# Channel attention: the negated, turned maxima are kept by ScalarE, between its exponentials, and counted on a semaphore of their own

## The reference, cut to what matters

```python
def _L1_xattn_ref(qkv, y):          # qkv: the layer-normed x, y: ctx_2048, both (32, 64, 256)
    N_HEADS = 16
    bs, width, length = qkv.shape   # 32, 64, 256
    ch = width // N_HEADS           # 4
    q = qkv.reshape(bs * N_HEADS, ch, length)
    k = v = y.reshape(bs * N_HEADS, ch, -1)
    scale = 1.0 / math.sqrt(math.sqrt(ch))
    weight = jnp.einsum('bct,bcs->bts', q * scale, k * scale)
    weight = jax.nn.softmax(weight.astype(jnp.float32), axis=-1).astype(weight.dtype)
    a = jnp.einsum('bts,bcs->bct', weight, v)
    return a.reshape(bs, -1, length)
...
    x = x + _L1_xattn_ref(_layernorm(x, axis=-1), ctx_2048)
```

## Time and profile before

| | us |
|---|---|
| median of 3 runs | 2005.89 (2004.52 to 2006.66) |
| the profiled execution, its own time | 2003.32 |
| its span, first to last instruction | 2001.5 |
| VectorE busy in the span | 1536.0 (77%) |
| TensorE busy (matmuls) | 1693.3 (85%) |
| ScalarE busy | 1030.8 (52%) |
| the reductions L1481, 256 of 1218 ns | 304.7 |
| the exponentials L1464, 512 of 598 ns | 278.6 |

### The profile page before, as it was taken

One profiled execution on the slowest core, in us unless ns is written; L12 is line 12 of the kernel. 1 busy time (PEld: TensorE's weight loads), 2 busy tenths in 40 slices (PEclk: granted clock), 3 DMA queues, 4 the chain that ended last, 5 costly groups with the idle time before them and its releaser, 6 DMA issues. The chain is left out here.

```text
span 2001.5 us, 43208 instructions
## 1 busy us (share of the span) xinstructions
PE 1693.3 (85%) x15683; PEld 999.4 (50%) x15744; DVE 1536.0 (77%) x2859; ACT 1030.8 (52%) x2056; POOL 741.9 (37%) x939
## 2 busy tenths in 40 slices
PE   5999999599999999787846763777777599999998
PEld 2665665267777677744424440222222146656565
DVE  5766666689989899669977987999999268675754
ACT  3666665255555555333316752888888333323222
POOL 4644321586777667387652333122221000000000
PEclk9999999799999999989979995999999799999999
DMA  9601000200000000011201111121211013222222
GB/s 240 165 28 49 28 7 2 62 14 9 15 12 9 6 9 1 22 53 54 63 16 33 40 29 30 47 62 53 58 55 40 24 39 92 90 70 69 67 78 53
DMA packets 86797, 94.91 MB, mean 47 GB/s; under 512 B 17472, under 2 KB 63168, under 8 KB 86592
## 3 DMA queue, kind: packets, MB, share of 16 engines
q1 hardware_dynamic: 82848, 87.76, 15.8%
q10 hardware_dynamic: 2976, 2.32, 0.5%
q0 software_dynamic: 768, 2.10, 0.4%
HBM read 78.51 MB, written 10.22 MB: 44 GB/s over the span
## 5 line engine op out<-in xcount | busy, mean ns | idle before, releaser
L205 PE MATMUL ps<-arena 128*128 128x512 f16 (+6 forms) x6403 | 1093.1, 324 | 81.1 <-POOL arena L1076 20.2
L205 PEld LDWEIGHTS ps<-arena 128*128 128x128 f16 (+1 forms) x6464 | 603.3, 99 | 471.1 <-issue 45.1
L1464 ACT ACTIVATE arena<-ps 128x512 f32<-128x512 f32 x512 | 278.6, 598 | 84.2 <-PE ps L1402 61.1
L1481 DVE TENSOR_REDUCE arena<-ps 128x4 f32<-128x1024 f32 x256 | 304.7, 1218 | 22.2 <-PE ps L1394 22.2
L1394 PE MATMUL ps<-arena 31*128 31x256 f16 x1024 | 103.5, 279 | 90.2 <-ACT arena L1464 53.6
L1449 PE MATMUL ps<-arena 128*32 128x256 f32 x2048 | 164.1, 392 | 2.6 <-ACT arena L1471 0.6
L2217 DVE TENSOR_TENSOR arena<-ps,arena 128x512 f32<-128x512 f32 x96 | 66.2, 690 | 117.5 <-ACT arena L2090 95.1
L2090 ACT ACTIVATE arena<-ps 128x512 f32<-128x512 f32 x96 | 57.2, 596 | 183.4 <-PE ps L205 183.1
L1394 PEld LDWEIGHTS ps<-arena 31*128 31x128 f16 x1024 | 34.9, 92 | 206.8 <-DVE arena L1481 153.0
L968 POOL TENSOR_TENSOR arena<-arena 128x512 f32<-128x512 f32 x96 | 98.6, 1041 | 44.8 <-DVE arena L156 43.7
L571 POOL TENSOR_TENSOR arena<-arena 128x256 f32<-128x256 f32 x64 | 39.2, 612 | 187.3 <-DVE arena L541 187.3
(11 more groups left out here) (200 smaller groups left out, 3009.0 us busy)
## 6 DMA issues: line engine op xcount, KB each, us to landing
arena<-moe_cw SPq DMA_DIRECT2D x64, 192.0 KB, 2.9
arena<-moe_cw SPq DMA_DIRECT2D x64, 128.0 KB, 3.0
arena<-in_L_ffn_gate_up_proj SPq DMA_DIRECT2D x12, 512.0 KB, 3.9
ch_out<-arena SPq DMA_DIRECT2D x32, 128.0 KB
arena<-moe_cw SPq DMA_DIRECT2D x64, 64.0 KB, 2.8
arena<-in_L_ffn_down_proj SPq DMA_DIRECT2D x6, 512.0 KB, 3.6
ch_keys<-arena SPq DMA_DIRECT2D x48, 64.0 KB, 2.0
arena<-ch_keys SPq DMA_DIRECT2D x64, 48.0 KB
```

Source lines behind the costliest of these rows:

```text
L205: last = nc.tensor.matmul(out, a, b, start=start and n == 0, stop=stop and n == len(pairs) - 1, skip_group_check=not group)
L1464: nc.scalar.activation(pT[:, b % 3, g], ps[:, T[n % len(T)], :].rearrange("p (u t) -> p u t", u=KD), ACT.Exp, scale=CH_SCALE).then_inc(s_e ...
L1481: nc.vector.tensor_reduce(m[:, half % 2, 2 * half_pair:2 * half_pair + 2, j, :], ps[:, bank(user):bank(user) + 2, :].rearrange("p g (u s) ...
```

## The change

The negation of the turned maxima leaves VectorE's list and enters ScalarE's, as a copy with scale -1. It counts on a new semaphore, `s_turned`; `s_maxed` counts reductions alone. A function `free` turns "user u is done with" into the right wait: for a turned user on `s_turned`, for the others on `s_maxed`, less the turned ones before it. SyncE's `load_max` waits for `s_turned`. ScalarE's loop begins two slots earlier, so that the copy of half h stands at slot b = 4h - 2, behind exponential g = 1.

```diff
+    turn_users = [a_turn(half) for half in range(CH_HALVES)]
+
+    def free(pe, user):
+
+        earlier = sum(u <= user for u in turn_users)
+        if user in turn_users:
+            pe.wait_ge(s_turned, earlier)
+        else:
+            pe.wait_ge(s_maxed, user + 1 - earlier)
@@ SyncE
             def load_max(half):
-                sp.wait_ge(s_maxed, a_turn(half) + 1)
+                sp.wait_ge(s_turned, half + 1)
@@ TensorE
                     user = (a_first, a_second)[pair](t)
                     if user >= 2:
-                        pe.wait_ge(s_maxed, user - 1)
+                        free(pe, user - 2)
...
                     user = a_turn(half)
-                    pe.wait_ge(s_maxed, max(user - 1, a_second(t - 1) + 1))
+                    free(pe, user - 2)
+                    free(pe, a_second(t - 1))
@@ ScalarE
-            for b in range(CH_SLOTS + CH_HALF):
+            for b in range(-2, CH_SLOTS + CH_HALF):
                 for g in range(CH_RGS):
-                    if b < CH_SLOTS:
+                    if 0 <= b < CH_SLOTS:
...
+                    half = (b + 2) // CH_HALF
+                    if g == 1 and (b + 2) % CH_HALF == 0 and half < CH_HALVES:
+                        user = a_turn(half)
+                        act.wait_ge(s_scored, user + 1)
+                        if half >= 2:
+                            act.wait_ge(m_in[half % 2], 16 * (half // 2))
+                        nc.scalar.activation(mT[:, half % 2], ps[0:32, bank(user), 0:P], ACT.Copy, scale=-1.0).then_inc(s_turned, 1)
@@ VectorE
                     top(a_first(t), t, 0)
-                if t % CH_HALF == 0 and t > 0:
-                    half = t // CH_HALF - 1
-                    user = a_turn(half)
-                    dve.wait_ge(s_scored, user + 1)
-                    if half >= 2:
-                        dve.wait_ge(m_in[half % 2], 16 * (half // 2))
-                    nc.vector.tensor_scalar(mT[:, half % 2], ps[0:32, bank(user), 0:P], -1.0, None, ALU.mult).then_inc(s_maxed, 1)
                 if t < CH_SLOTS:
                     top(a_second(t), t, 1)
```

More of the change, by code:

```diff
@@ L1291, in channel_stage @@
     s_norm, s_hi, s_lo, s_vset, s_ones, s_zero = (sem(c) for c in ("norm", "hi", "lo", "vset", "ones", "zero"))
-    s_scored, s_maxed, s_scoredT, s_exped, s_mixed, s_okept = (sem(c) for c in ("scored", "maxed", "scoredT", "exped", "mixed", "okept"))
+    s_turned, s_scored, s_maxed, s_scoredT, s_exped, s_mixed, s_okept = (sem(c) for c in ("turned", "scored", "maxed", "scoredT", "exped", "mixed", "okept"))
     s_inverse, s_divided, s_finished = sem("inverse"), sem("divided"), sem("finished")
```

## The result

The change makes the kernel slower, as forecast: 2023.26 us (2022.74 to 2026.09, 4 runs) against 2005.20 (2003.77 to 2006.66), ratio 1.0087 with a 95% interval of 1.0074 to 1.0100, that is 15 to 20 us. The forecast was 2025, 19 more than before.

A forecast was written before the change was run, and what follows sets the result against it. The prediction took the ScalarE-TensorE loop as the bound, with VectorE a close second. A delay of 0.63 us in 30 halves, 18.9, with 0 gained on VectorE, gave a median of 2025 us, range 2020 to 2032.

The forecast's parts named there:

- What bounds the stage: Channel stage: the closed ScalarE-TensorE-ScalarE loop sets 1.21 us steps; a bank-pair loop through VectorE's reduction sets the 1.71 long step.
- Taking the negation away gains 0: VectorE's long step: the 0.27 us negation is hidden by refilling the bank pair; gain 0 in each of 32 halves.
- The idle time that it leaves: VectorE before the reduction of step 145's scores: idle 0.57 us or so instead of 0.31 without the negation.
- The new wait: Step 146 waits for ScalarE's copy behind the second exponential: starts 1.85 us after step 145, not 1.21 or 1.22; delay 0.63.
- the lower bound, 0.06: Least latency from ScalarE's end to the matmul it releases, 0.06 us against 0.145 taken; delay then 0.55.
- 30 halves pay: Halves 1 to 30 of the channel stage each lose 0.63 us, 18.9 us in all; halves 0 and 31 do not.
- the 16.5 that I had as the least: Lower bound on the loss over the paying halves: 30 x 0.55 = 16.5 us.
- The transfer of the maxima is hidden: SyncE's transfer, released by the copy, lands about 4.05 us after step 145 began; step 149 needs it at 5.48.
- The total: Whole kernel: 18.9 us more, plus about 0.1 at the end; median 2025 us.
- VectorE as the bound: Rival: VectorE sets the channel stage's time, so removing the negation saves 8.6 to 18.6 us, 1987 to 1997; chance 0.03.
- The hidden copy: Rival: step 146 begins when the first exponential is done, as before, so nothing moves, 2006 us; chance 0.03.
- The clock: Rival: TensorE's granted clock falls through the new idle time, lengthening steps by some 0.2 us, 40 over the stage; chance 0.02.

The follow-up runs named there:

- waits_swapped: Kernel before with the two waits of each TensorE step swapped, exponentials first, then bank pair: 1997.9 us, ratio 0.9952 to before.
- tasks_in_gap: Changed kernel with ScalarE's copy two exponentials earlier and VectorE's reciprocal and statistics tasks moved into the negation's old place: 2002.8 us, ratio 0.9981 to before.
- copy_early: Changed kernel with ScalarE's copy of the turned maxima moved two exponentials forward: 2006.6 us, ratio 1.000 to before.
- after_waits_swapped: Changed kernel with the two waits of each TensorE step swapped, exponentials first, then bank pair: 2023.0 us, ratio 1.0076 to before.
- half_reduced: Kernel before with VectorE's reduction over only 128 of 256 keys: 1992.2 us, one run.
- neg_x4: Kernel before with VectorE's negation made four times, three into spare tiles: 2006.7 us, ratio 1.0005 to before.
- copy_x2: Changed kernel with ScalarE's copy made twice, the first into a spare tile: 2032.1 us, ratio 1.0121 to before.

## Why the prediction was right, point by point

- **What bounds the stage.** Right for the ordinary steps, and now shown: with reductions of 0.69 us the ordinary step is the same 1.213, and with 19 us more work on VectorE the stretch did not move. It is the loop from an exponential through TensorE to the next that counts; shortening it by 0.09 (waits_swapped) shortened the step by 0.086. The prediction read one half. In the middle of a tile, behind the statistics task, the long step is 1.956 and not 1.71, and there VectorE's work does count (tasks_in_gap took 3.3 us off the stretch). The change leaves these steps as they are, so the forecast did not suffer.
- **Taking the negation away gains 0.** Right: copy_early and before agree in the stretch to 0.1 us. The idle time that it leaves was misread: the records of the reduction and the negation overlap by 0.08, so it is 1407.12 - 1406.63 = 0.49, as measured, and not 0.57. Nothing in the sum hangs on it.
- **The new wait.** The mechanism and the place are right: the start of step 146 waits for the copy, which stands behind the second exponential. The terms, from the start of step 145 at 1418.87: the copy begins at 1.445 (predicted 1.445); it lasts 0.254 (0.26); from its end to the matmul it takes 0.056, where I had put 0.145. The step is 1.755, not 1.85, the delay 0.54, not 0.63. That is the one mis-sized term. I had taken the latency of "the same instruction", a score matmul; what decides is the place of the wait among the instruction's waits, as after_waits_swapped shows. The row for the lower bound, 0.06, was near the right size.
- **30 halves pay.** Right: 30 waits for the copy. Their sum is 15.8 (29 x 0.54 and 0.2) instead of 18.9, and under the 16.5 that I had as the least.
- **The transfer of the maxima is hidden.** Right: step 149 follows after 1.21, as before. The issue was at 1420.59, while the copy ended at 1420.57:

```profile
1420.59 0.59 SPq L1341 DMA_DIRECT2D arena<-arena  x1
```

- **The total.** 18.1 us by the medians, 16.7 in the stretch; 19 were forecast. The waits for the copy explain 15.8 of it. That the total came nearer to 19 is luck: 0.8 is the short fall of the clock in the one profiled execution, and the rest lies outside the stretch, where the start of the stage alone varies by 7 us between profiles.
- **The rivals.** VectorE as the bound has fallen by half_reduced and neg_x4, and so has, for this stage, the rule of the Trainium skill (Perfetto Trace Analysis, Identifying the Most-Contended Engine) that would have made it the forecast: occupancy was 97%, and neither 19 us more work nor reductions of little over half the length moved the ordinary step; only the long steps and the start of the stage gained by the shorter ones. The hidden copy exists, but two exponentials earlier (copy_early). The clock did fall once for 3.4 us, and that cost 0.8 us; a step that lay wholly in the fall was 0.35 longer, not the 0.2 that I had priced. Of the 13 profiles only two show such a fall between 1250 us and the last scores, the change and copy_x2, and both have the new pause in each half. after_waits_swapped has the pause too and shows none, and such falls come in other stages of every profile. So it is a hint, and I can't say that the pauses brought the fall on.

## What to carry to other kernels

Before moving work off a busy engine, look at what starts each of its instructions: if they begin a constant 0.04 us behind the matmul that feeds them, the engine follows there, and relief at that place is worth nothing; the time that work leaves can still be worth something as a place for tasks that do cost. A buffer's release belongs to the place in the new engine's list, not to the engine's load: here two exponentials further forward were the difference between 17 us and none. And where an instruction has several waits in the innermost loop, try the one that ends last in the first place, and waits that have long been fulfilled somewhere else: each time it was the trace of the new order that told what it was worth.

## What the runs showed of the hardware that I had not expected

- The order of two waits ahead of one TensorE matmul: from the end of a ScalarE instruction to the matmul it releases, 0.056 us if its wait is the first, 0.145 if it is the second, with the other long fulfilled. The same for VectorE's reduction in the long step: 0.057 before, 0.146 once swapped (1408.508 to 1408.654).
- Waits on transfers that had landed, standing ahead of the exponential's wait with the bank pair's behind it, raised the 0.056 to 0.100 (one of them) and to 0.256 (two, at a tile's start). Ahead of the values' matmuls they cost nothing. With the exponential's wait as the last of all it was 0.145, whether one, two or three waits stood ahead of it. Why the order matters no run here shows.
- Two ScalarE copies of 0.254 start 0.16 apart, two VectorE negations of 0.27 start 0.20 apart: a short task behind another costs less than its length. So sums of busy time overstate the work: in neg_x4 VectorE shows 10.23 busy of 10.23, and the half is 0.02 longer than the 10.21 of before.
- The releaser named in a row can mislead. In half_reduced TensorE's step at 1407.06 names VectorE's L1481. The reduction that its bank pair waits for is the one ahead of the row at 1406.27; by the same timeline it began at 1405.06 and lasted 0.69, so it had ended 1.3 us earlier; the step's length, unchanged when that reduction was halved, tells who it was.
